# A decoder of two layers on one core: expert gates loaded by token pairs, causal scores evicted by heads

## What is computed

```python
phi_q = relu(q) + 1e-3 ; phi_k = relu(k) + 1e-3
num_i = sum over j <= i of (phi_q_i . phi_k_j) v_j
den_i = sum over j <= i of (phi_q_i . phi_k_j)
out_i = num_i / den_i
```

```python
sx, ix = top_k(sim[0], 8) ; sy, iy = top_k(sim[1], 8)
scores, pk = top_k(sx[..., :, None] + sy[..., None, :], 8)   # of the 64 sums
indices = (ix * 64 + iy) at pk
h = gelu(x . down_embed[indices]) * softmax(scores)
out = sum over heads and picks of h * up_embed[indices]
```

## Time and profile before

| what | us |
|---|---|
| median of 3 runs (2892.51 to 2898.46) | 2892.74 |
| the profiled execution's own time | 2893.67 |
| its span in the profile | 2891.9 |
| TensorE busy | 2355.1 (81%) |
| VectorE busy | 1849.0 (64%) |
| ScalarE busy | 880.8 (30%) |
| GpSimd busy | 889.2 (31%) |
| experts stage, 2232 to 2875 | 643 |
| attention core, 1263 to 1364 | 101 |

### The profile page before, as it was taken

One profiled execution on the slowest core, in us unless ns is written; L12 is line 12 of the kernel. 1 busy time (PEld: TensorE's weight loads), 2 busy tenths in 40 slices (PEclk: granted clock), 3 DMA queues, 4 the chain that ended last, 5 costly groups with the idle time before them and its releaser, 6 DMA issues. The chain is left out here.

```text
span 2891.9 us, 33503 instructions
## 1 busy us (share of the span) xinstructions
PE 2355.1 (81%) x12062; PEld 1578.2 (55%) x12062; DVE 1849.0 (64%) x4585; ACT 880.8 (30%) x1791; POOL 889.2 (31%) x503
## 2 busy tenths in 40 slices
PE   7666666798974795787896778789798899999996
PEld 3222222433664795355473444337466788888885
DVE  5899999724641523557325996532687866667764
ACT  1365565413832420101422333041222211111110
POOL 0198898503504953100102333422100211011000
PEclk9899999999986897799997888889898999999997
DMA  3100000000022463100101000020200000000000
GB/s 100 40 0 0 1 0 1 1 9 1 1 97 77 166 222 95 56 1 2 36 0 35 1 1 1 0 72 0 117 1 5 1 1 1 1 1 1 1 1 30
DMA packets 48666, 84.99 MB, mean 29 GB/s; under 512 B 6802, under 2 KB 38290, under 8 KB 47124
## 3 DMA queue, kind: packets, MB, share of 16 engines
q1 hardware_dynamic: 46964, 78.64, 8.2%
q0 software_dynamic: 1536, 4.20, 0.5%
HBM read 73.13 MB, written 9.44 MB: 29 GB/s over the span
## 5 line engine op out<-in xcount | busy, mean ns | idle before, releaser
L748 PE MATMUL scan_YP<-scan_H,ident 128*128 128x512 f32 x512 | 260.6, 633 | 129.1 <-POOL scan_H L721 116.1
L721 POOL TENSOR_TENSOR scan_H<-scan_H,scan_CS 128x1024 f32<-128x1024 f32 x128 | 300.9, 2352 | 46.5 <-DVE scan_H L816 46.5
L816 DVE TENSOR_TENSOR_SCAN scan_H<-scan_AB,XT 128x512 f32<-128x512 f32 x256 | 298.2, 1207 | 0.0
L2382 PE MATMUL ex_HP<-XT,pe_DOWN 128*128 128x256 f32 x1024 | 239.7, 389 | 11.9 <-PEq L2230 6.6
L748 PEld LDWEIGHTS scan_YP<-scan_H,ident 128*128 128x128 f32 x512 | 89.3, 194 | 278.2 <-POOL scan_H L721 197.0
L2412 PE MATMUL ex_OP<-pe_UP,ex_GH 128*128 128x256 f32 x1024 | 238.4, 396 | 1.3 <-DVE ex_GH L2569 1.3
L776 ACT ACTIVATE scan_AB<-mamba_E,mamba_AA 128x510 f32<-128x510 f32 x256 | 194.3, 775 | 100.0 <-DVE scan_H L816 99.8
L2412 PEld LDWEIGHTS ex_OP<-pe_UP,ex_GH 128*128 128x128 f32 x1024 | 203.2, 200 | 31.1 <-DVE ex_GH L2569 1.5
L2382 PEld LDWEIGHTS ex_HP<-XT,pe_DOWN 128*128 128x128 f32 x1024 | 195.0, 195 | 40.3 <-ACT ex_GH L2441 8.1
L2441 ACT ACTIVATE ex_GH<-ex_HP 128x512 f32<-128x512 f32 x128 | 76.2, 601 | 462.3 <-PE ex_HP L2382 334.5
L2569 DVE SCALAR_TENSOR_TENSOR ex_GH<-ex_GP,ex_GH 128x1024 f32<-128x1024 f32 x64 | 78.4, 1225 | 169.3 <-issue 151.1
(11 more groups left out here) (415 smaller groups left out, 4670.9 us busy)
## 6 DMA issues: line engine op xcount, KB each, us to landing
moe_W<-in_L_ffn_w SPq DMA_DIRECT2D x32, 1024.0 KB, 7.5
pe_DOWN<-in_L_ffn_down SPq DMA_DIRECT2D x1, 4096.0 KB, 12.7
pe_UP<-in_L_ffn_up SPq DMA_DIRECT2D x1, 4096.0 KB, 23.1
moe_dispatch<-route_ZERO SPq DMA_DIRECT2D x1, 2560.0 KB, 8.7
experts_XE<-moe_dispatch SPq DMA_DIRECT2D x16, 160.0 KB, 2.4
moe_answers<-experts_YE SPq DMA_DIRECT2D x16, 160.0 KB, 3.0
XT<-in_xT SPq DMA_DIRECT2D x1, 2048.0 KB, 7.6
X<-in_x SPq DMA_DIRECT2D x1, 2048.0 KB, 11.8
```

The source lines that it names most:

```text
L721: pool.tensor_tensor(H[:, m % RING], H[:, m % RING], over(CS[:, r % 2], 2), ALU.mult).then_inc(hc_ready, 1)
L748: ins = pe.matmul(YP[:, c, :], ident[:, 0:P], H[:, m % RING, i], start=(s == 0), stop=(s == DS - 1))
L816: v.tensor_tensor_scan(H[:, m % RING, i], AB[:, n % 2, :], BU[:, r % 2, c], 0.0, ALU.mult, ALU.add).then_inc(h_ready, 1)
L2382: ins = pe.matmul(HP[:, n % 2, a, :], DOWN[:, k, 2 * q + a, :], XT[:, k, b * BLK:(b + 1) * BLK], start=(k == 0), stop=(k == KD - 1))
```

## The change

**Attention core.** The evictions are split by heads. VectorE takes heads 0 and 1, all three tiles in one product with a mask of three tiles (triangle, ones, triangle: the new input `causal`, 128 columns wider than `tri`). ScalarE copies heads 2 and 3 unmasked (`rest`), and GpSimd then multiplies their two diagonal tiles by the triangle in place. The scores of turn m wait for `masked` and `rest_copied`, the outputs for `masked` and `rest_masked`. On TensorE the transposes come ahead of the outputs. The two divisions become one instruction.

**Experts.** The picks of a token no longer stand twice. Partitions 0 to 63 hold the picks of one token, 64 to 127 those of the token 64 further on in the same tile; both have one load. The moving operand R is block-diagonal: for the first token only its 64 partitions are filled, for the second only the others, and each has a high and a low part side by side: 2 tokens x 2 parts x 32 = 128 columns. The other half is zeroed once. High and low gates now stand in different columns of `GP` and are added on the way out: ScalarE copies the low ones, scaled, into the new `GS` (`low_gates`), VectorE adds the high ones and then multiplies `GH` (`gate`). A unit has 16 positions of pairs, of which a step takes 8 (16 tokens): `gates`, `hid`, `low_gates` and `gate` go by steps, 128 of them. `answer` is cut into 8 parts of 4 matmuls, one a step. `KEYS`, `DUP` and the transposes are f16, 16 small ones of 64 x 64 a block. `ranks` moves from unit 1 to unit 2.

The attention core:

```diff
@@ performer_core
+    HALF = LHC // 2
...
                 def outs(m):
                     pe.wait_ge(masked, m + 1)
+                    pe.wait_ge(rest_masked, m + 1)
...
                     if m:
                         pe.wait_ge(masked, m)
+                        pe.wait_ge(rest_copied, m)
...
                     ins.then_inc(scores_ready, 1)
+                    if m >= 2:
+                        turn(m - 2)
                     if m >= 1:
                         outs(m - 1)
-                    if m >= 2:
-                        turn(m - 2)
...
+                def rest(m):
+                    act.wait_ge(scores_ready, m + 1)
+                    if m >= 2:
+                        act.wait_ge(out_ready, m - 1)
+                    act.activation(A[:, m % 2, HALF:LHC].rearrange("p h a q -> p h (a q)"), SC[:, HALF:LHC, 0:3 * P], ACT.Copy).then_inc(rest_copied, 1)
...
+                for m in range(NU):
+                    rest(m)
+                    if m:
+                        out_copy(m - 1)
+                out_copy(NU - 1)
...
+            @block.gpsimd
+            def _(pool):
+                for m in range(NU):
+                    pool.wait_ge(rest_copied, m + 1)
+                    corners = A[:, m % 2, HALF:LHC, 0:3:2, :]
+                    tri = MASK[:, 0, :].rearrange("p (h a q) -> p h a q", h=1, a=1).to_broadcast([P, LHC - HALF, 2, P])
+                    pool.tensor_tensor(corners, corners, tri, ALU.mult).then_inc(rest_masked, 1)
...
-                    v.tensor_tensor(a[:, :, 0, :], sc[:, :, 0, :], tri, ALU.mult)
-                    v.tensor_tensor(a[:, :, 2, :], sc[:, :, 2, :], tri, ALU.mult)
-                    v.tensor_copy(a[:, :, 1, :], sc[:, :, 1, :]).then_inc(masked, 1)
+                    v.tensor_tensor(A[:, m % 2, 0:HALF].rearrange("p h a q -> p h (a q)"), SC[:, 0:HALF, 0:3 * P],
+                                    MASK[:].rearrange("p (o a) q -> p o (a q)", o=1).to_broadcast([P, HALF, 3 * P]), ALU.mult).then_inc(masked, 1)
```

The experts:

```diff
@@ peer_experts
-    RING = NP + 2
+    RING = NP + 1
+    HALF = P // 2
+    POS = UNIT // 2
+    STEP = POS // 2
+    UT = P // UNIT
+    PARTS = 2 * UT
+    JP = J2 // PARTS
...
-        L = st.sb("L", [P, 2, P, UNIT], F16)
-        R = st.sb("R", [P, 2, J2, UNIT], F16)
+        L = st.sb("L", [P, 2, P, POS], F16)
+        EQ = st.sb("EQ", [P, J2, POS], F16)
+        R = st.sb("R", [P, 2, 2, 2, J2, POS], F16)
+        GS = st.sb("GS", [P, 2, J2, STEP, 2])
...
+                def gates(i):
+                    n = i // 2
                     pe.wait_ge(left_ready, n + 1)
                     pe.wait_ge(right_ready, n + 1)
+                    if i >= 2:
+                        pe.wait_ge(gated, i - 1)
+                    for x in range(STEP):
+                        t = i % 2 * STEP + x
+                        ins = pe.matmul(GP[:, i % 2, x].rearrange("p h x j -> p (h x j)"), L[:, n % 2, :, t],
+                                        R[:, n % 2, :, :, :, t].rearrange("p h x j -> p (h x j)"), start=True, stop=True)
...
+                for i in range(2 * NU):
+                    b, q = divmod(i, 2 * UB)
+                    gates(i)
+                    if i > PARTS:
+                        answer((i - 1) // PARTS - 1, (i - 1) % PARTS)
                     if b + 1 < NB:
+                        hid(b + 1, q)
+                        if q == TURN_AT * PU + PU - 1:
                             turn(b + 1)
...
+                def low_gates(i):
+                    act.wait_ge(gates_ready, i + 1)
+                    if i >= 2:
+                        act.wait_ge(gated, i - 1)
+                    low = GP[:, i % 2].rearrange("p t h x j -> p j (t h) x")[:, :, :, 1]
+                    act.activation(GS[:, i % 2].rearrange("p j t h -> p j (t h)"), low, ACT.Copy, scale=1.0 / PSCALE).then_inc(low_copied, 1)
...
-                    ch.link(v.tensor_tensor(runs(R[:, n % 2]), numbers(J2), runs(along(1, J2)), ALU.is_equal))
+                    ch.link(v.tensor_tensor(runs(EQ[:]), numbers(J2), runs(along(1, J2)), ALU.is_equal))
                     v.tensor_tensor(runs(L[:, n % 2]), numbers(P), runs(along(0, P)), ALU.is_equal).then_inc(left_ready, 1)
-                    v.tensor_tensor(R[:, n % 2], R[:, n % 2], along(2, J2), ALU.mult).then_inc(right_ready, 1)
+                    for h in range(2):
+                        rows = slice(h * HALF, (h + 1) * HALF)
+                        both = KEYS[rows, b % 2, 2:4, a, pos].rearrange("p q (o t) -> p q o t", o=1).to_broadcast([HALF, 2, J2, POS])
+                        ins = v.tensor_tensor(R[rows, n % 2, h], EQ[rows].rearrange("p (o j) t -> p o j t", o=1).to_broadcast([HALF, 2, J2, POS]),
+                                              both, ALU.mult)
+                    ins.then_inc(right_ready, 1)
...
+                def gate(i):
+                    v.wait_ge(low_copied, i + 1)
+                    high = GP[:, i % 2].rearrange("p t h x j -> p j (t h) x")[:, :, :, 0]
+                    gs = GS[:, i % 2].rearrange("p j t h -> p j (t h)")
+                    ch.link(v.scalar_tensor_tensor(gs, high, 1.0 / PSCALE, gs, ALU.mult, ALU.add))
+                    gh = GH[:, b % 2, :, a * P:(a + 1) * P].rearrange("p j (h t) -> p j t h", h=2)[:, :, at:at + STEP, :]
+                    v.tensor_tensor(gh, GS[:, i % 2], gh, ALU.mult).then_inc(gated, 1)
```

More of the change, by code:

```diff
@@ L2387, in turn @@
                     pe.wait_ge(arranged, b + 1)
-                    for part, qs in ((0, (0, 1)), (1, (2,))):
-                        n = turn_place(b, part)
-                        pe.wait_ge(hidden_read, n - 1)
-                        for q in qs:
-                            for a in range(TB):
-                                ins = pe.transpose(HP[:, n % 2, q % 2, a * P:(a + 1) * P], DUP[:, q, a].rearrange("p a k -> p (a k)"), ident[:, 0:P])
-                        ins.then_inc(hidden, 1)
@@ L2396, in gates @@
-                def gates(n):
+                    n = turn_place(b)
+                    pe.wait_ge(hidden_read, n - 1)
+                    turned = HP[:, n % 2].rearrange("p s (q a k) -> p (s q) a k", a=TB, k=HALF)
+                    for q in range(4):
+                        for a in range(TB):
+                            for h in range(2):
+                                rows = slice(h * HALF, (h + 1) * HALF)
+                                ins = pe.matmul(turned[rows, q, a, :], DUP[rows, q, a, :], I16[rows, rows], start=True, stop=True)
@@ L2397, in gates @@
+                    ins.then_inc(hidden, 1)
+                def gates(i):
+                    n = i // 2
                     pe.wait_ge(left_ready, n + 1)
                     pe.wait_ge(right_ready, n + 1)
-                    if n >= 2:
-                        pe.wait_ge(gated, n - 1)
-                    for t in range(UNIT):
-                        ins = pe.matmul(GP[:, n % 2, t, :], L[:, n % 2, :, t], R[:, n % 2, :, t], start=True, stop=True)
+                    if i >= 2:
[4 more added lines that the diff above has]
+                                        R[:, n % 2, :, :, :, t].rearrange("p h x j -> p (h x j)"), start=True, stop=True)
@@ L2403, in gates, with answer @@
                     ins.then_inc(gates_ready, 1)
-                def answer(m):
+                def answer(m, part):
                     b, a = m // TB, m % TB
-                    pe.wait_ge(gated, (m + 1) * P // UNIT)
-                    if m >= 2:
-                        pe.wait_ge(out_read, m - 1)
-                    for j in range(J2):
+                    if part == 0:
+                        pe.wait_ge(gated, (m + 1) * PARTS)
+                        if m >= 2:
+                            pe.wait_ge(out_read, m - 1)
+                    for j in range(part * JP, (part + 1) * JP):
@@ L2550, in select_step @@
                         pick(b, u)
-                        if u == TB - 1:
-                            ranks()
+                    elif u == TB:
+                        ranks()
                     elif u == 3:
@@ L2556, in select_step @@
                         probabilities(b)
+                v.tensor_copy(I16[:], ident[:, 0:P]).then_inc(ident_ready, 1)
+                for h in range(2):
+                    ch.link(v.memset(R[(1 - h) * HALF:(2 - h) * HALF, :, h], 0.0))
                 v.wait_ge(loaded, 32)
@@ L2565, in _ @@
                         sides(n + 1)
-                    v.wait_ge(gates_ready, n + 1)
-                    v.wait_ge(hidden_read, (b + 1) * RING)
-                    gh = GH[:, b % 2, :, u * UNIT:(u + 1) * UNIT]
-                    v.scalar_tensor_tensor(gh, GP[:, n % 2].rearrange("p t j -> p j t"), 1.0 / PSCALE, gh, ALU.mult, ALU.mult).then_inc(gated, 1)
-                    if n % (P // UNIT) == 2 and n > P // UNIT:
-                        answer_out(v, n // (P // UNIT) - 1)
+                    for half in range(2):
+                        gate(2 * n + half)
+                    if n % UT == 0 and n > UT:
```

(2 more changed lines are left out.)

97 lines of the change are left out of this document (51 added, 46 removed).

## The result

The changed kernel is slower: **2926.47 us** (2924.62 to 2928.27, four runs) against 2894.95 us (2892.51 to 2898.46, four runs) for the kernel before, ratio 1.0108, 95% interval 1.0090 to 1.0125. The forecast was 2831 us. The profiled execution of the changed kernel took 2926.29 us, with a span of 2924.5.

What follows compares the result with a forecast made beforehand. The prediction took TensorE to bound the experts and the eviction wait on the single score buffer the attention core. 2893.7 - 25 (attention core) - 37 (experts) = 2831.7, so a median of 2831 us; range 2806 to 2866.

Steps and rivals of the forecast that it cites:

- Experts, TensorE: Experts stage: 2048 gate matmuls of 32 columns become 1024 of 128 at 69 ns, 71 us replacing 141.
- load and columns add: Upper bound for one gate matmul in the experts: weight load plus streaming, 69 + 96/2.4 = 109 ns.
- the scan pair: Two bf16 matmuls of 512 columns, different weights, starting 0.22 us apart; taken as evidence that the weight load is hidden.
- Attention core, -25: Attention core: split evictions cut a turn from 2.99 to 2.15 us, saving 25 us; ends -29 and +8.
- rival 1: Experts' gate matmuls: weight load not hidden, 109 ns each, some +20 us, 2851 us; chance 0.15.
- rival 2: Experts: VectorE loses its double rate in products on half the partitions, a block 5 us more, 2867 us; chance 0.08.
- the unit's terms: Experts, VectorE's work per unit: left side, equality, probabilities and gating, summed to 5.8 us, up 0.7.
- The product of 512 at 0.69: Experts' gating on VectorE: each addition or product of 512 f32 elements takes 0.69 us.
- Rival 3: Experts: VectorE's f32 operations on SBUF held by GpSimd or the gated tile's stride, 2.6 us a step, 2926 us; chance 0.05.
- Who sets the block: Experts: VectorE sets the five units with selection, TensorE the other three; 73 us a block, stage -37 us.
- The clock stays: Experts, TensorE: the granted clock would hold, as it was still 1.00 with TensorE busy 4.27 of 6 us.
- The other signs: Experts: VectorE's share rises from 72% to over 85%; TensorE waits for left and right sides only in units with selection.

Runs made afterwards that it cites:

- pairs: Changed kernel with neighbouring tokens paired, so the gated tile is read in runs of 16 values; moving operand still 32 bytes apart: 2925.58 us, ratio 1.0112.
- mov1_gh: mov1 with a step's 16 tokens side by side in the gated tile GH (other values): 2788.5 us, ratio 0.9692 to the kernel before.
- mov1: Changed kernel with the gate matmuls' 128 moving columns read side by side instead of 32 bytes apart (other values): 2832.57 us, ratio 0.9778.

## Why the prediction was wrong

**The step that failed is the price of the gate matmul**, in "Experts, TensorE": 1024 x 69 ns = 71 us, bounds 69 and 109. It took 237 ns, 243 us in all: 172 us more of TensorE than forecast, of which 95 show in the time, since the forecast had left TensorE room behind VectorE. The upper bound was "load and columns add", which presumes one column a cycle. Every row under it came from operands whose moving values lie side by side: the scan pair, the key scores, the transposes. The gates' own row was the exception, 32 columns 64 bytes apart in 69 ns, and it could not show the pace, since 4 x 13.3 = 53 ns stays under the 60 or so that hold it anyway. Four cycles a column fit that row as well as one does, and would have given 4 x 53 = 213 ns for 128 columns: an upper bound of 213 or more was there to be read from the layout and the row together. With 237 ns, TensorE's unit is 2 x 5.37 = 10.7 us against a forecast of 8.1, over VectorE's everywhere, and the block is 16 x 5.37 + 0.4 = 86.3, as measured.

Point by point:
- **Attention core, -25:** right in mechanism, measured -31. The turn was 2.07 us, not 2.15; it was the arithmetic's 2.06 and the margin for GpSimd wasn't needed, though GpSimd took 1.27 us and not 1.1. 31 x 0.92 = 28.5 us by the turns, the rest at the ends of the stage.
- **"The load is not hidden" (rival 1):** refuted. 55 ns with both operands side by side; the bf16 pair of the earlier trace rows was the right witness.
- **VectorE keeps its double rate (against rival 2):** mostly right. The products on 64 partitions took 0.77 us, mean, with 0.69 taken; the equality took 0.42 as forecast. The left side took 1.31, not 1.2. Two sums are off without weight here: the unit's terms add up to 5.7 us and not 5.8, and rival 2's price leaves out the last block, 8 x 1.1 = 9 us.
- **The product of 512 at 0.69:** wrong, 1.11. It was named as what would make the forecast wrong, and it did not: hidden in the changed kernel (pairs), worth 20 to 25 us once the gates are repaired (mov1_gh against mov1). Rival 3 had the cause as one of two ("the stride of the gated tile") with a price of 1.3 us a step; it cost 0.4. That its 2926 equals the result is chance: VectorE wasn't the bound.
- **Who sets the block:** the prediction's 73 us, set by VectorE in the units with selection, appears as soon as the stride is gone: 74.5 in mov1, and 71.9 in mov1_gh, where the product has its 0.69. The time of mov1, 2832.6, matches the forecast of 2831, in part because the attention core, better by 6 us than forecast, stands against the slower product.
- **"The clock stays":** right for the changed kernel (1.00 in the block), not for mov1 (0.95 with TensorE busy 68 of 74.5 us, where a block before had 0.98).
- **The other signs:** VectorE's share did not rise to 85% (79%), and TensorE waited 6.6 us for the gating in the whole stage. "It would be wrong if the halved gates left TensorE busy all through" is what happened.

That the cost follows the distance of the moving values, in doublings, is shown by five distances with the rest unchanged. How the chip fetches them is not.

## What to carry to other kernels

Before a matmul gets more columns, look at how far apart its moving values lie in their partition: here f16 values up to 4 bytes apart streamed at about one a cycle, 8 bytes apart at two cycles each and 16 or 32 at four (61, 66, 118, 231 and 237 ns for 128), and a matmul of 32 columns showed only 6 ns of it. A bound taken from another row holds only for that row's layout; when the columns grow, price the layout at its worst. And one surplus on an engine hides the next: repair the bound first, then cost what was hidden by it.

## What the hardware showed that was not expected

- **The moving operand's distance:** 61, 66, 118, 231, 237 ns for 128 f16 columns at 2, 4, 8, 16, 32 bytes. The Trainium skill ("Advanced Engine Details and Errata", SBUF Cachelines) wants two hits on a 16-byte line for full pace. Values 8 bytes apart have two and already take 118 ns, so this trace does not agree for TensorE's moving operand. From 16 bytes to 32, neither with two hits, little is added (231 and 237).
- **The stationary operand's distance hardly matters:** 32 bytes apart cost 6 to 8 ns a load (61 to 55, 237 to 229).
- **VectorE in f32 cares too:** a product of 512 takes 0.69 us in runs of 16 values and 1.10 where the innermost two lie 256 bytes apart. In f16, runs of two in place of 16 cost the equality 0.62 us against 0.42.
- **TensorE's clock:** the changed kernel, with TensorE busy through the block, has 1.00. With pauses behind VectorE between 2250 and 2700 us (up to 5.4 us in mov1, 3.0 in mov1_gh), four blocks of mov1 have 0.98, 0.95, 0.95 and 0.98, and four of mov1_gh 0.95, 1.00, 1.00 and 0.98. So in these traces the clock is below 1.00 only in blocks where TensorE pauses, but not in all of them; what decides it wasn't tried.
